# A state-space mixer with gated experts: one schedule of the mixer's steps exchanged for another on five engines

## What is computed

```
xn = layernorm(x)
out = x + mixer(xn) + experts(xn)

mixer:  z, xBC, dt = split(xn @ in_proj.T);  dt = softplus(dt + dt_bias)
        xBC = silu(causal_conv4(xBC) + conv_b)          # x_ssm 512, B 64, C 64
        theta = clip(theta_base + tanh(xn @ w1) @ w2, -pi/2, pi/2)
        lambda_eff = lambda_base + eta * theta**2
        log_z = complex(-lambda_eff * dt, theta * dt)   # per head and state block
        per chunk of 64 tokens: S_total = exp(cumlog) * state + intra-chunk sum
                                y = real(C . S_total);  state = S_total[last]
        g = (y + x_ssm * D) * silu(z)
        mixer = (g * rsqrt(mean(g*g) + eps) * norm_w) @ out_proj.T
experts: the softmax's top expert of 8: gate * (xn @ W[e] + b[e])
```

## Time and profile before

| | |
|---|---|
| median of 3 runs | 1141.43 us (1137.7 to 1141.64) |
| span of the profiled execution | 1132.4 us |
| mixer, from its first mask to the end | 286.4 to 1132.4 us |
| TensorE busy | 990.2 us, 87% of the span |
| VectorE busy | 956.0 us, 84% |
| ScalarE busy | 843.9 us, 75% |
| GpSimd busy | 419.7 us, 37% |

### The profile page before, as it was taken

How to read it: one execution, slowest core, us unless ns; L and a number is a source line. 1 busy time by engine, 2 the same in 40 slices (tenths; PEclk the granted TensorE clock), 3 DMA queues, 4 the chain that set the end, 5 groups by cost and what they waited for, 6 DMA issues and landing times.

```text
span 1132.4 us, 25279 instructions
## 1 busy us (share of the span) xinstructions
PE 990.2 (87%) x8700; PEld 804.9 (71%) x8700; DVE 956.0 (84%) x1485; ACT 843.9 (75%) x1710; POOL 419.7 (37%) x413
## 2 busy tenths in 40 slices
PE   4962889677899999999999999999999999999994
PEld 2532677455687887888787778787878787787774
DVE  5848623269999999999999999999999999999961
ACT  4944212059698888888888888888889898888871
POOL 2200777110334343424334433434343434342542
PEclk9985799879899999999999999999999999999997
DMA  7969566433456565656564656566555656565552
GB/s 246 327 227 371 152 214 199 113 87 127 139 152 172 145 187 148 186 153 181 151 183 137 184 150 189 152 171 165 153 166 152 180 146 191 147 180 150 175 164 40
DMA packets 150372, 194.00 MB, mean 171 GB/s; under 512 B 20990, under 2 KB 110511, under 8 KB 148832
## 3 DMA queue, kind: packets, MB, share of 16 engines
q1 hardware_dynamic: 114752, 146.70, 38.3%
q0 software_dynamic: 24960, 34.62, 16.3%
q10 hardware_dynamic: 10528, 11.01, 2.9%
HBM read 75.99 MB, written 40.63 MB: 103 GB/s over the span
## 4 chain that ended last, share of the span: by engine, by line
DVE 44%; PE 13%; issue 11%; SPq 4%; ACT 3%; DMA 3%; POOL 1%; DVEq 0%; POOLq 0%; ACTq 0%
DVE conv L1250 11%; DVE att L1337 4%; PE ps L863 3%; PE ps L985 3%; DVE prod L1320 3%; DVE prod L1319 3%; DVE prod L1310 2%; DVE lam L1284 2%; SPq L787 2%; DVE bup L1330 2%; DMA rep<-bc_d 2%; DVE prod L1309 2%; DVE angle L1276 2%; PE ps L943 2%; DVE g L1355 2%
## 5 line engine op out<-in xcount | busy, mean ns | idle before, releaser
L863 PE MATMUL ps<-xn_in,win 128*128 128x256 f32 x1152 | 284.0, 393 | 7.5 <-issue 3.5
L863 PEld LDWEIGHTS ps<-xn_in,win 128*128 128x128 f32 x1152 | 214.4, 194 | 43.8 <-issue 11.7
L1411 POOL TENSOR_TENSOR state_in<-state,cin_s 128x256 f32<-128x256 f32 x56 | 53.7, 959 | 325.6 <-DVE state L1345 325.6
L1250 DVE SCALAR_TENSOR_TENSOR conv<-x_pre,col,conv 128x512 f32<-128x512 f32 x240 | 161.5, 743 | 10.6 <-ACT conv L1058 10.6
L985 PE MATMUL ps<-wout,g 128*128 128x256 f32 x512 | 128.3, 395 | 17.5 <-DVE g L1355 17.4
L985 PEld LDWEIGHTS ps<-wout,g 128*128 128x128 f32 x512 | 96.2, 196 | 36.8 <-DVE g L1355 24.9
L1438 POOL TENSOR_TENSOR rms<-ms,cst 128x1 f32<-128x1 f32 x64 | 68.2, 1066 | 119.2 <-ACT ms L1164 119.2
L1418 POOL DMA_INDIRECT plus_tile<-expert_d,slot_of x64 | 91.0, 1422 | 44.7 <-DMA out<-plus_tile 35.1
L531 POOL DMA_INDIRECT r_tiles<-xn_d,token_of x72 | 68.7, 954 | 70.7 <-POOLq L397 48.5
L972 PE MATMUL ps<-att,x_tok 128*64 128x128 f32 x1024 | 71.7, 283 | 25.2 <-DVE att L1337 25.2
L1337 DVE TENSOR_TENSOR att<-ps,cst 128x1024 f32<-128x1024 f32 x64 | 78.0, 1218 | 18.4 <-PE ps L947 18.4
(11 more groups left out here) (170 smaller groups left out, 2316.2 us busy)
## 6 DMA issues: line engine op xcount, KB each, us to landing
cin_s<-cin SPq DMA_DIRECT2D x128, 129.0 KB, 2.6
rep<-bc_d SPq DMA_DIRECT2D x128, 128.0 KB, 3.3
grow_s<-grow SPq DMA_DIRECT2D x128, 128.0 KB, 3.4
cown_s<-cown SPq DMA_DIRECT2D x128, 128.0 KB, 2.1
bup_s<-bup SPq DMA_DIRECT2D x128, 128.0 KB, 2.3
expert_d<-r_tiles ACTq DMA_DIRECT2D x18, 512.0 KB, 3.3
xn_d<-r_tokens SPq DMA_DIRECT2D x16, 512.0 KB, 4.3
xnT_d<-r_turned SPq DMA_DIRECT2D x4, 2048.0 KB, 24.2
```

Of the source, the lines that this page charges most:

```text
L863: last = nc.tensor.matmul(dst, win[:, kt, n * P:(n + 1) * P], xn_in[b][:, kt, :], start=(kt == 0), stop=(kt == KT - 1))
L1250: nc.vector.scalar_tensor_tensor(conv[:, ct, :], x_pre[:, ct, tap:tap + PT], c("conv_w", ct * D_CONV + tap), conv[:, ct, :], ALU.mult, ALU ...
```

## The change

The step functions stay as they are, line by line. Only the order of the calls changes, in the prologue and in the body, on all five engines. No step is added or removed over the whole run, so the work is the same. The body on VectorE and SyncE:

```diff
-                    front_conv(m + 2, 10, 15)
-                    front_waves(m + 1)
+                    front_lamdt(m + 2)
                     back_mask(m, 0)
-                    front_lamdt(m + 2)
                     front_cin(m + 1)
                     back_gate(m, 0)
+                    front_frac(m + 2)
+                    back_state(m, 0)
                     back_mask(m, 1)
-                    front_decay(m + 2)
-                    back_state(m, 0)
                     front_bup(m + 1)
-                    front_frac(m + 2)
                     front_cown(m + 1)
                     front_conv(m + 3, 0, 6)
                     front_conv(m + 3, 6, 10)
+                    front_decay(m + 2)
                     back_gate(m, 1)
+                    back_state(m, 1)
                     front_clip(m + 3)
-                    back_state(m, 1)
+                    front_conv(m + 3, 10, 15)
+                    front_waves(m + 2)
                     front_phase(m + 3)
...
                 for m in range(MACROS):
-                    load_xn(m + 4)
-                    stack_grow(m + 1)
-                    load_dt(m + 3)
-                    load_hidden(m + 3)
-                    stack_cin(m + 1)
-                    stack_bup(m + 1)
-                    bounce(m + 2)
-                    stack_cown(m + 1)
-                    replicate(m + 2)
+                    bounce(m + 3)
+                    load_dt(m + 4)
+                    stack_cin(m + 2)
                     store(m, 0)
+                    stack_bup(m + 2)
+                    stack_cown(m + 2)
+                    load_hidden(m + 6)
                     store(m, 1)
+                    replicate(m + 3)
+                    stack_grow(m + 3)
+                    load_xn(m + 6)
```

142 lines of the change are left out of this document (83 added, 59 removed).

## The result

The changed kernel takes 1155.6 us in the median (1151.2 to 1157.8), the kernel before 1140.7 us beside it: ratio 1.0138, 95% interval 1.0114 to 1.0163. It is slower, where 1127 us (1113 to 1139) were predicted.

The account below looks back on a forecast made before the run. VectorE and TensorE are both nearly full, so neither alone was taken as the bound. Span 1132.4 - 12.6 (loop) + 3.2 (ahead) - 5.0 (behind) = 1118.0 us, or 1127.0 us for the median, range 1113 to 1139.

Parts of the forecast that it names:

- Contention on VectorE: Loop: moving the state sums ahead of mask and theta stops GpSimd's product slowing VectorE, saving 0.87 us per iteration.
- the two near ties with TensorE: Short iteration: gate of half 0 and mask of half 1 come just as TensorE finishes; 0.5 us together.
- Rep: Long iteration: VectorE and ScalarE's bpart wait for the copies into rep; 0.5 us for both, VectorE's wait 0 to 2.
- Rep becomes the wait: Rival: late rep landings, or load_hidden holding SyncE, cost long iterations 1.7 us more in most pairs; 1139 us, chance 0.13.
- The issue: SyncE's queue: hidden's load and a store delay rep 0.6 us each, bounce gives 0.6 back; rep 0.6 us later.
- The landing: Copies into rep land 2.5 to 5.2 us after issue, as in the kernel before; median 3.3 us.
- TensorE's bound: Loop pair: 51.2 us visible work plus a new 1.4 us bank wait at front_z_a; 52.6 us, setting the long iteration's pace.
- The loop: 14 pairs of a short and a long iteration fall from 53.7 to 52.8 us each, saving 12.6 us.
- Ahead of the loop: Before the loop: SyncE's new order delays dt and xn loads, lamdt(2) moves forward; +3.2 us, bounds 0 and +6.
- Behind iteration 28: End of kernel: the epos stall falls to some 0.2 us and contention losses go; -5.0 us, bounds -2 and -8.
- The contention only moves: Rival: GpSimd's product starts late behind rms, DMA and gather, and meets bup and angle again; 1135 us, chance 0.12.
- TensorE's clock: Rival: the new 1.4 us wait drops TensorE's clock in each long iteration; 14 falls cost 25 us, 1152 us, chance 0.06.

Follow-up runs that it names:

- e5_sums_back: Changed kernel with VectorE's two sums of the state back where they stood before; ratio to before 1.0176 (1.0149 to 1.0203).
- e10_rms_shifted: Kernel before with both sums of the state moved, plus a 64-column memset ahead of the last five conv steps; ratio to before 0.9934.
- e1_sums_only: Kernel before with only VectorE's two sums of the state moved, ahead of the mask and of theta; ratio to before 1.0127.
- e6_dt_early: Changed kernel with replicate directly behind stack_cown and the load of dt at the end of SyncE's body; ratio to before 0.9996.
- e13_rep_free: Changed kernel with replicate behind stack_cown, the load of dt at SyncE's body end, and back_add_x ahead of GpSimd's half 1 product; ratio to before 0.9990.
- e7_z_behind_out: e6_dt_early with TensorE's front_z_a moved behind front_turn and back_out; ratio to before 1.0135 (1.0109 to 1.0161).
- c3_before_neutral: Kernel before with only SyncE's last two waits, behind the whole loop, in the other order; ratio to before 0.9994.

## Why the prediction was wrong, by its steps

**Contention on VectorE: mechanism and size right.** Product 0.62 us, bup 0.68, scans 1.39 (1.3 named), which is 0.43 + 0.31 = 0.74 us where 0.87 were taken. The short iteration came out at 20.4 us, even below the 21.0 predicted: the two near ties with TensorE cost nothing. What failed is the step from "VectorE works 0.87 us less" to "the pair gets shorter". In the new order it is worth nothing (e5_sums_back), since VectorE only arrives earlier at rep. In the old order it is worth 0.7% (e10_rms_shifted), and turns into a loss where it moves rms (e1_sums_only).

**Rep: the step that failed.** The prediction took 0.5 us per long iteration, bounds 0 to 2. It was 37.0/14 = 2.6 us, beyond the bound, and the rival "Rep becomes the wait" had the right mechanism with chance 0.13. Its size was wrong in two places, here in medians over the long iterations from 360 to 1040 us.

The issue: rep's first DMA starts 2.6 us behind the end of cown in the kernel before and 4.3 us in the changed one, 1.7 us later where 0.6 were taken. The load of hidden and the store cost 1.1 us, as foreseen. But the 0.6 us that `bounce` was to give back don't exist: in the kernel before SyncE mostly starts on cown 0.08 us behind its end, so `bounce` held nothing up (the 0.77 us of the earlier trace rows is one of two such delays in 13), and in the changed kernel it starts on it 0.55 us behind. Rep's four issues take 2.6 us in both; the 3.10 us in the rows further up are not typical.

The landing: it was taken from the kernel before, though the change also moved three DMAs of GpSimd beside it, and the four of grow_s behind it (whose share was not separated). From the end of the issues to VectorE's start there pass 5.2 us, where before the last copy had landed after 4.0. The 3.3 us that the prediction used are the median over all copies; the last of the four ahead of a long iteration took 4.6 us from its own issue already in the kernel before.

With VectorE wanting rep 9.4 and 9.3 us behind the end of cown, that makes 2.6 + 2.6 + 4.0 = 9.2 us before, 0.2 us to spare, and 4.3 + 2.6 + 5.2 = 12.1 us after, a wait of 2.8. The prediction listed each DMA that SyncE's queue puts ahead of rep, and none that runs at the same time from another queue. The stall of 0.81 us was one of 5 in the 14 long iterations (of 2 on the quick chip), but with 0.2 us to spare in the others the slack was as good as used up: nearly the whole sum counts.

The rival named a second way, `load_hidden` holding SyncE. It happened, 11 waits for theta of 17.0 us in all from 360 to 1040 us, but ahead of the other rep, that of the short iterations, for which VectorE comes 10.0 us behind the issues and never waits.

**TensorE's bound: right, not reached.** 52.6 us were worked out for TensorE's pair, with the new wait of 1.4 us for the bank (measured 1.36, in each long iteration). The changed kernel never got there. With rep in time long iterations took 32.1 us and the best pairs 20.5 + 32.1 = 52.6 us (e6_dt_early, e13_rep_free). The traces also show why the new order then gains nothing. In the kernel before TensorE is not idle at all in a long iteration of 31.07 us, and idle for 2.3 us in a short one of 22.05 (medians). In e13_rep_free the long iteration has TensorE's wait of 1.35 us and takes 32.1, the short one has 0.2 us of idle time and takes 20.8. What the short iteration gains, the wait for the bank takes back in the long one, where TensorE was full already. The run that removed this wait lost the clock (e7_z_behind_out), so its price of 1 us a pair is read and not tested.

**The loop.** -12.6 us predicted; +13.0 us measured between the two profiles from quick chips (14 x 0.93).

**Ahead of the loop: right.** +3.2 us predicted, +3.0 us measured (63.5 against 60.5; +1.9 in the first profiles). VectorE's wait for dt of iteration 1, of after:

```profile
266.24 0.69 DVE L1279 TENSOR_TENSOR angle<-theta,dt_in 128x512 f32<-128x512 f32 x1 [3.25 <-DMA dt_in<-dtT_d]
```

**Behind iteration 28: wrong.** -5.0 us predicted (bounds -2 to -8), +3.3 us measured on quick chips (+2.1 in the first profiles). This part varies by itself: in c3_before_neutral, whose loop is that of before, it took 96.0 us, as long as in the changed kernel, and 92.5 to 96.0 us over the four profiles of the old order. So the gain of 5 us did not come, but a loss is not shown. The stall at epos did fall, to 1.02 us, but not to 0.2. The masks of the last two iterations then waited for scores, 3.88 and 7.23 us, where in the kernel before they waited 0.41 and 4.82:

```profile
1126.37 1.23 DVE L1354 TENSOR_TENSOR att<-ps,cst 128x1024 f32<-128x1024 f32 x1 [7.23 <-PE ps L960]
```

```profile
1123.65 1.16 PE L956 MATMUL ps<-cown_s,grow_s 64*128 64x128 f32 x16 [1.52 <-DMA cown_s<-cown]
```

The prediction removed stalls there without asking what comes next. That the end of cown decides the last masks is read from these two rows; no run tested it.

**The other rivals.** "The contention only moves" was right in kind for the sums alone, through rms and not through the product; in the changed kernel rms takes 1.24 us in the mean against 1.08, but ScalarE waits only 1.8 us for it in all. "TensorE's clock" did not happen: none of the 70 stretches of the changed kernel is below 1.00, with a wait of 1.36 us between long products in each pair. It did happen in e7_z_behind_out, by two shorter waits around one-column products.

The Trainium skill, "SBUF — State Buffer", section "Who interferes with whom", says that a VectorE instruction with at most one SBUF input, outside its two-port modes, does not contend with GpSimd. The products beside a mask or theta agree, at 0.61 to 0.69 us in the changed kernel. The same section of the Trainium skill says that whoever comes first holds the shared ports for its whole instruction. The product agrees with that: it starts 0.42 us ahead of the second bup sum and takes 0.4 us longer than alone, as if it had waited for the first sum to end, and the second sum grows by as much. Rms does not fit: it was held over four VectorE operations and not one.

## What to carry to other kernels

Time saved on a full engine is worth only what the next arrival allows: before pricing it, find for each of its waits how late the data already is, and count every DMA in flight beside it, from all queues, not only those ahead in the same queue. Where two engines slow each other, moving an operation out of one collision moves the rest of the schedule by tenths of a microsecond into others; look at the smallest operations of the other engine on the path, not only at the large ones. Spans from different chips can differ by 11 us in untouched code, so compare the start of the part that is changed first.
